# Denominators of a joint classifier made once, in the head, by fp32 matmuls

## What is computed

```
v0, v1, v2, v3 = softmax of each quarter (16 wide) of the logits, 512 rows
flat[b, (i, j, c, d)] = v0[b,i] * v1[b,j] * v2[b,c] * v3[b,d]          # 512 x 65536
num_y_joint[y, J] = sum over b of flat[b, J] * y_true[b, y]            # 100 classes
num_joint[J]      = sum over b of flat[b, J]                           # the denominators
prob_y_joint = clip(max(num_y_joint, 1e-6) / max(num_joint, 1e-6), 0, 1)
probs[b, y] = sum over J of prob_y_joint[y, J] * flat[b, J]            # 512 x 100
```

## Time and profile before

| | |
|---|---|
| median of 3 runs | 584.12 us (584.08 to 584.28) |
| span of the profiled execution | 582.4 us |
| TensorE matmul | 539.0 us busy, 93% of the span |
| VectorE | 345.8 us, 59% |
| GpSimd | 135.8 us, 23% |
| ScalarE | 55.7 us, 10% |
| mean granted TensorE clock | 0.982 |

### The profile page before, as it was taken

One profiled execution on the slowest core, in us unless ns is written; L12 is line 12 of the kernel. 1 busy time (PEld: TensorE's weight loads), 2 busy tenths in 40 slices (PEclk: granted clock), 3 DMA queues, 4 the chain that ended last, 5 costly groups with the idle time before them and its releaser, 6 DMA issues.

```text
span 582.4 us, 10067 instructions
## 1 busy us (share of the span) xinstructions
PE 539.0 (93%) x3088; PEld 302.5 (52%) x3088; DVE 345.8 (59%) x735; ACT 55.7 (10%) x119; POOL 135.8 (23%) x96
## 2 busy tenths in 40 slices
PE   4777887579999999999999999999999999999996
PEld 2343443235555555555555555555555555555553
DVE  7899999996673644444454644445354644445445
ACT  4445454000001000000001000000001000000000
POOL 4899999990001300000001300000001300000000
PEclk9999998988999999999999999999999999999999
DMA  2111110000000000000000000000000000000000
GB/s 75 42 54 37 54 36 0 0 0 0 0 0 1 1 0 0 0 0 0 0 0 0 0 0 0 0 0 0 0 0 0 0 0 1 0 0 0 0 0 14
DMA packets 3013, 4.57 MB, mean 8 GB/s; under 512 B 816, under 2 KB 1072, under 8 KB 3008
## 3 DMA queue, kind: packets, MB, share of 16 engines
q1 hardware_dynamic: 2480, 4.30, 2.3%
q10 hardware_dynamic: 528, 0.20, 0.1%
HBM read 4.27 MB, written 0.24 MB: 8 GB/s over the span
## 4 chain that ended last, share of the span: by engine, by line
PE 77%; DVE 16%; issue 4%; DVEq 1%; ACT 1%; DMA 0%; POOL 0%; ACTq 0%; POOLq 0%
PE numbers L442 13%; PE numbers L443 13%; PE numbers L444 13%; PE joined L452 12%; PE joined L454 12%; PE joined L453 12%; DVE p_lo L351 9%; DVE r_hi L371 2%; DVE ratio L366 2%; DVEq L351 1%; DVE acc L406 1%; DVE inv L364 1%; ACT p_hi L281 0%; DVE qf L188 0%; DVE den L361 0%
## 5 line engine op out<-in xcount | busy, mean ns | idle before, releaser
L442 PE MATMUL numbers<-q_hi,p_hi 128*128 128x404 f16 (+1 forms) x508 | 172.7, 340 | 22.2 <-DVE p_lo L351 22.2
L452 PE MATMUL joined<-r_hi,pt_hi 128*128 128x400 f16 x512 | 170.9, 334 | 7.8 <-DVE r_lo L373 7.7
L443 PE MATMUL numbers<-q_lo,p_hi 128*128 128x404 f16 (+1 forms) x508 | 171.9, 338 | 0.0
L444 PE MATMUL numbers<-q_hi,p_lo 128*128 128x404 f16 (+1 forms) x508 | 171.8, 338 | 0.0
L453 PE MATMUL joined<-r_lo,pt_hi 128*128 128x400 f16 x512 | 170.7, 333 | 0.0
L454 PE MATMUL joined<-r_hi,pt_lo 128*128 128x400 f16 x512 | 170.5, 333 | 0.0
L361 DVE TENSOR_SCALAR den<-numbers 128x4 f32<-128x4 f32 x128 | 20.5, 160 | 211.2 <-PE numbers L444 209.9
L373 DVE SCALAR_TENSOR_TENSOR r_lo<-ratio,r_hi 128x400 f16<-128x400 f32 x128 | 99.5, 778 | 4.4
L442 PEld LDWEIGHTS numbers<-q_hi,p_hi 128*128 (+1 forms) x508 | 50.0, 98 | 63.7 <-issue 28.0
L258 POOL TENSOR_TENSOR qg<-qf,v0f 128x1600 f32<-128x1600 f32 x3 | 8.6, 2862 | 303.6 <-ACT qf L313 303.6
L452 PEld LDWEIGHTS joined<-r_hi,pt_hi 128*128 (+1 forms) x512 | 50.0, 98 | 50.4 <-issue 14.3
(11 more groups left out here) (53 smaller groups left out, 115.2 us busy)
## 6 DMA issues: line engine op xcount, KB each, us to landing
v1b<-v_rows SPq DMA_DIRECT2D x15, 256.0 KB, 3.2
labels<-in_r_y_true_dram ACTq DMA_DIRECT2D x1, 200.0 KB, 2.9
out_dram<-acc SPq DMA_DIRECT2D x1, 200.0 KB, 2.0
x<-in_r_logits_dram SPq DMA_DIRECT2D x1, 128.0 KB, 2.2
v_rows<-v1t SPq DMA_DIRECT2D x1, 32.0 KB, 1.6
```

The lines of the kernel that those rows point to most:

```text
L442: pe.matmul(out, hi, qh, start=(k == 0), stop=False)
L443: pe.matmul(out, hi, ql, start=False, stop=False)
L444: last = pe.matmul(out, lo, qh, start=False, stop=(k == KC - 1))
L452: pe.matmul(out, hi, r_hi[:, slot, :], start=first, stop=False)
```

## The change

The labels lose their column of ones: `labels` is 4 x 100 wide, NW becomes 400, and the memset of that column and the waits on it go. The denominators of all 128 steps are made in the head: GpSimd makes `v01` = v0 x v1 (four instructions of 256 elements) behind its half of q; TensorE multiplies it by each half of p23, in fp32, four matmuls of 256 columns for each half, between count(0, 0) and count(0, 1), into the banks of joined 2 and 3; VectorE clips each of the two results into `den`, ordered by step, and makes the reciprocals of the first 128 elements ahead of its loop and those of the other 384 behind it. The two small instructions in make_ratios are gone. `v01` lies in `qg`, so GpSimd waits for the eight matmuls before it makes the q of group 1.

```diff
-    CW = CLASSES + 1
-    NW = AG * CW
     PW = AG * CLASSES
+    NW = PW
+    STEPS = GROUPS * TILES
...
-        labels = sb("labels", [LANES, KC, CW], FP32)
+        labels = sb("labels", [LANES, KC, CLASSES], FP32)
...
+        v01 = qg[:, 0:KC * S * S].rearrange("p (k j i) -> p k j i", k=KC, j=S)
...
-        den = sb("den", [LANES, SLOTS, AG], FP32)
-        inv = sb("inv", [LANES, SLOTS, AG], FP32)
+        den = sb("den", [LANES, STEPS * AG], FP32)
+        inv = sb("inv", [LANES, STEPS * AG], FP32)
...
+        den_psum = [joined[2], joined[3]]
...
-            pool.memset(labels[:, :, CLASSES:CW], 1.0).then_inc(ones_set, 1)
...
             pool.tensor_tensor(q_lo[:, QH:QW], qf[:, QH:QW], q_hi[:, QH:QW], ALU.subtract).then_inc(q0_right_lo, 1)
+
+            for k in range(KC):
+                last = pool.tensor_tensor(v01[:, k, :, :],
+                                          vk[:, k, 1, :].unsqueeze(2).broadcast_to([LANES, S, S]),
+                                          vk[:, k, 0, :].unsqueeze(1).broadcast_to([LANES, S, S]), ALU.mult)
+            last.then_inc(v01_made, 1)
...
+            pool.wait_ge(den_ready, 2)
             with pool.Fori(1, GROUPS) as g:
...
-                dve.tensor_scalar(den[:, slot, :], got[:, :, CLASSES], STABLE, 1.0 / UP, ALU.max,
-                                  ALU.mult).then_inc(den_made, 1)
-                dve.wait_ge(den_made, step + 1)
-                dve.reciprocal(inv[:, slot, :], den[:, slot, :]).then_inc(inv_made, 1)
-                dve.wait_ge(inv_made, step + 1)
                 dve.scalar_tensor_tensor(ratio[:, slot, :].rearrange("p (a y) -> p a y", a=AG),
-                                         got[:, :, 0:CLASSES], STABLE,
-                                         inv[:, slot, :].unsqueeze(2).broadcast_to([LANES, AG, CLASSES]),
+                                         got, STABLE,
+                                         inv[:, bass.ds(step * AG, AG)].unsqueeze(2).broadcast_to([LANES, AG, CLASSES]),
                                          ALU.max, ALU.mult).then_inc(ratio_made, 1)
...
+            def make_den(h):
+
+                dve.wait_ge(den_ready, h + 1)
+                den_by_step = den[:, :].rearrange("p (g j h a) -> p g j h a", g=GROUPS, j=S, h=2)[:, :, :, h, :]
+                got = den_psum[h][:, 0:S * S].rearrange("p (j g a) -> p g j a", j=S, g=GROUPS)
+                dve.tensor_scalar(den_by_step, got, STABLE, 1.0 / UP, ALU.max, ALU.mult).then_inc(den_made, 1)
...
             make_p_lo(0, 0, 1)
             make_p_lo(0, 1, 2)
+            make_den(0)
+            make_den(1)
+            dve.wait_ge(den_made, 2)
+            dve.reciprocal(inv[:, 0:TILES * AG], den[:, 0:TILES * AG]).then_inc(inv_made, 1)
+            dve.wait_ge(inv_made, 1)
             with dve.Fori(1, S) as i:
                 make_ratios(2 * i - 2, 0)
                 make_p_lo(i, 0, 2)
                 make_ratios(2 * i - 1, 1)
-            STEPS = GROUPS * TILES
+            dve.reciprocal(inv[:, TILES * AG:], den[:, TILES * AG:]).then_inc(inv_made, 1)
+            dve.wait_ge(inv_made, 2)
...
             last.then_inc(numbers_ready, 1)
+
+            for h in range(2):
+                pe.wait_ge(v01_made, 1)
+                for k in range(KC):
+                    last = pe.matmul(den_psum[h][:, 0:S * S], p23[:, k, h * HALF:(h + 1) * HALF],
+                                     v01[:, k, :, :].rearrange("p j i -> p (j i)"), start=(k == 0), stop=(k == KC - 1))
+                last.then_inc(den_ready, 1)
             pe.wait_ge(p_ready, 2)
             count(0, 1, 1)
...
+            pe.wait_ge(den_made, 2)
             join(0, 0, 0, first=True)
```

More of the change, by code:

```diff
@@ L108, in joint_classifier @@
         v1_first = joined[1]
+        den_psum = [joined[2], joined[3]]
         logits_in = sem("logits_in")
         labels_in = sem("labels_in")
-        ones_set = sem("ones_set")
+        v01_made = sem("v01_made")
+        den_ready = sem("den_ready")
         ident_set = sem("ident_set")
@@ L185, in v0_times_y @@
         def v0_times_y(eng, out, k0, k1, group):
-            v0g = vk[:, k0:k1, 0, bass.ds(AG * group, AG)].unsqueeze(3).broadcast_to([LANES, k1 - k0, AG, CW])
-            yg = labels[:, k0:k1, :].unsqueeze(2).broadcast_to([LANES, k1 - k0, AG, CW])
+            v0g = vk[:, k0:k1, 0, bass.ds(AG * group, AG)].unsqueeze(3).broadcast_to([LANES, k1 - k0, AG, CLASSES])
+            yg = labels[:, k0:k1, :].unsqueeze(2).broadcast_to([LANES, k1 - k0, AG, CLASSES])
             return eng.tensor_tensor(out.rearrange("p (k a y) -> p k a y", k=k1 - k0, a=AG), v0g, yg, ALU.mult)
@@ L199, in _ @@
             pool.wait_ge(labels_in, 16)
-            pool.wait_ge(ones_set, 1)
             v0_times_y(pool, qf[:, QH:QW], KC // 2, KC, 0).then_inc(q0_right, 1)
@@ L374, in make_ratios @@
                                          ALU.min, ALU.subtract).then_inc(ratios_ready, 1)
+            def make_den(h):
[3 more added lines that the diff above has]
+                dve.tensor_scalar(den_by_step, got, STABLE, 1.0 / UP, ALU.max, ALU.mult).then_inc(den_made, 1)
             make_p23(0)
             dve.wait_ge(labels_in, 16)
-            dve.wait_ge(ones_set, 1)
             v0_times_y(dve, qf[:, 0:QH], 0, KC // 2, 0).then_inc(q0_left, 1)
```

## The result

The changed kernel takes 587.6 us (587.3 to 588.2), the kernel before 584.1; the ratio is 1.0071, with an interval from 1.0051 to 1.0092. The profiled execution took 588.2 us and spans 586.4. The executions of the kernel before lie in two groups in every comparison (in those of the experiments 29 at 582.1 to 582.7 us and 27 at 583.8 to 585.0, and the profiled one is of the upper group), so a difference under 2 us is read from traces, not from medians.

A forecast was written before the change was run, and what follows sets the result against it. GpSimd's head work, taking turns with VectorE, plus TensorE's remaining work set the time. 582.4 + 8.2 + 0.5 - 0.5 - 0.22 - 2.75 - 0.2 = 587.4, with 1.7 outside the span 589.1 us; range 582.5 to 592.0.

The forecast's parts named there:

- A whole value behind, +8.2: Head: VectorE falls one value i, 8 turns, behind; two counts and two joins more are left for TensorE, +8.2 us.
- The stall: Head: VectorE stands 9.4 us before its first ratio, which starts at 25.5 us where it started at 16.1.
- v01 in turns with q_lo and p_lo: Head: v01's four GpSimd instructions, 0.75 us each, alternate with VectorE's q_lo and p_lo; fourth p_lo done at 17.7 us.
- fp32 matmuls at 3.4 us full and 6.8 us half: Head, TensorE: eight fp32 matmuls take 3.4 us at full clock, 6.8 at half; taken as 4.3, mostly full clock.
- Clip and reciprocals: VectorE: clip 0.42 us, first reciprocals 0.95 before the first ratio, the other 384 2.5 us behind tile 29, costing nothing.
- Four columns, -2.75: TensorE-bound stage: some 110 counts, each four columns narrower, give back 0.025 us each, -2.75 us.
- Lateness, -0.5: Head: without den and inv, r_hi is no longer late, 0 to 0.06 us per set over 19 sets; -0.5 us taken.
- The end, -0.22: Very end: TensorE's 0.22 us wait on r_lo before its last pass goes away, -0.22 us.
- A: Rival: VectorE's own chain sets the head, so each removed den and inv shortens it, 7.4 us; 583.1 us, chance 0.17.
- B: Rival: head work hides in GpSimd's pause, fp32 matmuls at full clock, stall 4.4 us; 584.1 us, chance 0.15.
- C: Rival: half clock lasts for all eight fp32 matmuls, v01 1.03 us each, stall 13 us; 593 us, chance 0.08.

The follow-up runs named there:

- no_pair: Kernel before with den and inv taken out of make_ratios, the ratio reading a constant, 404 columns kept: 585.1 us, ratio 1.0031.
- one_more: Kernel before with one more four-element reciprocal in every set, into an unread buffer; it overlapped and did not lengthen the stretch: 583.3 us, ratio 0.9999.
- half_ptf: Kernel before with GpSimd's 32 ptf products cut to 256 of their 512 columns, VectorE's and TensorE's instructions unchanged: 566.9 us, ratio 0.9723.
- pair_back: Changed kernel with a four-element den and its reciprocal put back into every set, into unread buffers: 590.7 us, ratio 1.0122.
- mm_only: Changed kernel with v01 filled with a constant instead of the four GpSimd products; fp32 matmuls, clip and reciprocals kept: 586.3 us, ratio 1.0056.
- no_head: Changed kernel without its head work (no v01, fp32 matmuls, clip or long reciprocals), inv a constant, 400 columns: 581.4 us, ratio 0.9957.

## Why the prediction was right, step by step

*A whole value behind, +8.2.* Right: p_lo(9) ends where p_lo(10) did. The stall was 10.1 us (16.1 to 26.2), of which 0.9 is a later start of everything (below); 9.4 were forecast.

*v01 in turns with q_lo and p_lo.* Right as to the turns, too dear in size: the four take 3.64 us, 0.91 each with their turns, where 4.6 were forecast. TensorE could go on at 16.86 (17.7 forecast); without the later start that is a delay of 2.5 us against 4.3.

*fp32 matmuls at 3.4 us full and 6.8 us half.* The price was right, the share wrong. Each matmul has two records; near 19 us they start 0.43 us apart, and from 22.7 us on the trace has the full clock. So about four and a half of eight ran at 0.85 us and the rest at 0.43: 5.4 us, against the 4.3 that I took. From 16.86 to the first ratio it is 9.3 us, 7.8 forecast. So the stall came out near the forecast because three errors nearly cancelled: v01 1.8 us too dear, what follows it 1.5 us too cheap, and the later start not foreseen. That part is luck.

*Clip and reciprocals.* 0.42, 0.95 and 2.55 us; forecast 0.42, 0.95 and 2.5. By these times the 6.2 ns an element of the rows hold, and the estimate of 8.3 ns from the count of 8 in the Trainium skill, page VectorE: DVE Perf Modes, section First, the fixed hardware budget, was a third too high. The first ratio waits a further 0.36 us behind the reciprocal, where I had 0.1 for all waits. TensorE has no gap at the second reciprocal, as forecast.

*Four columns, -2.75.* Two steps take 8.12 us (142.72 to 150.84) against 8.17 in the kernel before: 0.025 a count, as taken.

*Lateness, -0.5.* Not there, in this kernel or in `no_pair`.

*The end, -0.22.* Right: the last matmuls of TensorE start 0.17 us apart throughout, the wait on r_lo is gone.

*What was not in the sum: the clock.* The kernel before ran at half clock when its TensorE stage began, and the changed kernel did not. Busy time of TensorE alone in the kernel before, and of all engines in the changed one (the column that stands behind the busy times is the granted clock):

```profile
132.00:133.00 1.00, 1.00 (x4) 0.54 0.00 0
133.00:134.00 1.00, 1.00 (x5) 0.50 0.00 0
134.00:136.00 2.00, 2.00 (x9) 0.63 0.00 0
```
```profile
132.00:133.00 1.00, 0.76 (x5) 0.48 (x6) 0.95 (x3) 0.00 (x0) 0.00 (x0) 1.00 0.00 0
133.00:134.00 1.00, 1.00 (x8) 0.57 (x7) 0.58 (x1) 0.00 (x0) 0.00 (x0) 1.00 0.00 0
134.00:136.00 2.00, 2.00 (x14) 1.14 (x13) 1.33 (x3) 0.00 (x0) 0.00 (x0) 1.00 0.00 0
```

18 matmuls against 27 in the same 4 us, 1.5 us given back. The forecast had no term for it, so this is luck. That is the difference between 587.4 forecast for the span and 586.4, together with the 0.5 us of lateness on the other side. `no_pair` shows the reverse: it ran at half clock from 131.2 to 138.0, and is slower than the kernel before though VectorE's head ended at the same time. `one_more` shows it best, since its sets are as long as those of the kernel before: in its trace p_lo(10) ends at 131.9 as well, no half clock follows up to 140 us, and the span is 580.8 us against 582.4. The two groups of the kernel before go with the clock too: 24 of the 29 lower executions have a granted clock of 0.989 or 0.991, and all upper ones 0.982 to 0.988. Against the lower group the changed kernel is 5 us slower, not 3.5.

The rivals: A fell, by r_hi, by the sets of `no_pair` and by `half_ptf`; `pair_back` suggests where it would begin. B fell by the 5.17 us of the p_lo, by the half clock of the fp32 matmuls and by `mm_only`, which has neither and is still at 586.3 us. (The 0.43 us that I gave r_lo there is what it still runs after GpSimd's instruction; undisturbed it takes 0.58, at 178.17 in the changed kernel.) C did not occur: about half of the matmuls ran at half clock, not all. On A the Trainium skill, page SBUF — State Buffer, section Who interferes with whom, says that an instruction of VectorE with two inputs in SBUF contends with one of GpSimd that reads SBUF, and one with at most one such input does not, outside the two-port modes. The traces agree: p_lo and r_lo waited, and the ratio, with one of its two inputs in PSUM, took at most 0.58 us in all 14 traces. r_hi has one input in SBUF and waited too (0.83 us), so by the page it would run in a two-port mode, which no run here shows by itself.

## What to carry to other kernels

Where VectorE and GpSimd take turns, what VectorE does between its turns was free here while it fitted beside GpSimd's instruction (1.0 us), so taking small instructions out of it did not shorten a set; where this cover ends was not measured closely. Holding VectorE up costs turns, and most of them did not come back. Before moving work into a head, look for who waits behind it and for a pause of the same engine later on: here matmuls for three quarters of the same columns fitted into TensorE's pauses 50 us and more later. Before explaining 1 or 2 us, look where the half clock lies in each trace. And long instructions on GpSimd beside a critical VectorE are worth more attention than VectorE's own.

## What the runs showed that I had not expected

The rows of the labels, 100 elements end to end in place of 100 of 101, change when the logits land. In the changed kernel and in `label_stride`:

```profile
3.92 0.42 DVE L330 TENSOR_REDUCE stat<-x 128x16 f32<-128x256 f32 x1 [3.92 <-DMA x<-in_r_logits_dram]
```
```profile
2.91 0.42 DVE L330 TENSOR_REDUCE stat<-x 128x16 f32<-128x256 f32 x1 [2.91 <-DMA x<-in_r_logits_dram]
```

```diff
-        labels = sb("labels", [LANES, KC, CLASSES], FP32)
+        labels = sb("labels", [LANES, KC, CLASSES + 1], FP32)
...
-            yg = labels[:, k0:k1, :].unsqueeze(2).broadcast_to([LANES, k1 - k0, AG, CLASSES])
+            yg = labels[:, k0:k1, 0:CLASSES].unsqueeze(2).broadcast_to([LANES, k1 - k0, AG, CLASSES])
```

> The changed kernel, but a row of labels is again 101 elements wide in SBUF (the last one is never read), so the transfer of the labels has its former packets. In the changed kernel and in no_head, whose rows are 100 wide and lie end to end, the logits landed 0.9 us later than in the kernels with 101. If the packets of the label transfer do that: the logits land after 2.2 us again in place of 3.2 and the time is 0.9 us lower, 586.7 us. If it is chance: the landing varies in both and the time stays at 587.6.

The landing is what was expected, and it holds in every trace: VectorE starts at 2.8 to 3.0 us in the eight kernels with 101, at 3.8 to 3.9 in the six with 100. The labels' queue has 528 packets with the one and 144 with the other. The time went the other way: 589.1 us, ratio 1.0098 (1.0079 to 1.0118), 1.5 us above the changed kernel. The first ratio is at 23.6 us, 2.6 us sooner (1.0 by the landing, the rest because all but the first of the fp32 matmuls ran at full clock), but p_lo(8) and p_lo(9) both fell beside the q instructions (9.45 and 8.55 us a group), and TensorE was at half clock from 127.8 to 134.6. So 2.6 us at the start of this head are worth less than where VectorE stands when GpSimd's q instructions begin, and than the clock.
